# A macaron block on one core: waits between scattered stores, and the order of the router's steps around attention and the first shared products

## The reference, cut to what matters

```python
x = x + 0.5 * ffn(layernorm(x))
x = x + attention(layernorm(x))          # chunked gated linear attention, 2 heads of 128
x = x + 0.5 * ffn(layernorm(x))

def ffn(x):                              # 1024 tokens of 256 values
    shared = (silu(x @ g.T) * (x @ u.T)) @ down.T * sigmoid(x @ sgate.T)   # 704 hidden
    p = softmax(x @ gate.T)              # 16 experts
    w, ids = top_k(p, 4)
    return shared + sum over the 4 chosen experts e of  w_e * expert_e(x)  # 176 hidden
```

## Time and profile before

| | us |
|---|---|
| median of 3 runs | 455.74 (454.93 to 457.75) |
| the profiled execution's own time | 455.48 |
| its span, from first to last instruction | 453.7 |

### The profile page before, as it was taken

One profiled execution on the slowest core, in us unless ns is written; L12 is line 12 of the kernel. 1 busy time (PEld: TensorE's weight loads), 2 busy tenths in 40 slices (PEclk: granted clock), 3 DMA queues, 4 the chain that ended last, 5 costly groups with the idle time before them and its releaser, 6 DMA issues.

```text
span 453.7 us, 8744 instructions
## 1 busy us (share of the span) xinstructions
PE 410.8 (91%) x2236; PEld 330.4 (73%) x2239; DVE 300.4 (66%) x943; ACT 202.1 (45%) x564; POOL 188.9 (42%) x199
## 2 busy tenths in 40 slices
PE   5998993699999999978969989689989999999995
PEld 3555552599999999553649975355569999999954
DVE  5666986377777776367596545645767777777637
ACT  2224562266666666124755632001126666666610
POOL 0174846044445445330055300767514544544542
PEclk9988997699999999989998976989999999999999
DMA  7999941344444441660000029422244444444167
GB/s 248 332 281 386 344 136 66 105 136 139 136 148 137 138 144 66 245 252 2 0 0 1 1 73 372 170 104 103 79 119 137 136 138 148 132 145 141 68 242 258
DMA packets 41023, 68.17 MB, mean 150 GB/s; under 512 B 5072, under 2 KB 32208, under 8 KB 40976
## 3 DMA queue, kind: packets, MB, share of 16 engines
q1 hardware_dynamic: 33392, 45.84, 32.4%
q0 software_dynamic: 7584, 21.77, 13.6%
HBM read 42.42 MB, written 25.17 MB: 149 GB/s over the span
## 4 chain that ended last, share of the span: by engine, by line
PE 70%; issue 7%; POOL 6%; DVE 6%; DMA 6%; ACT 3%; SPq 1%; DVEq 0%; POOLq 0%
PE ps L486 7%; PE ps L487 7%; PE ps L490 7%; POOL slots L907 6%; PE ps L426 6%; PE ps L449 5%; PE ps L471 5%; PE ps L431 4%; PE ps L519 3%; PE ps L514 2%; PE ps L518 2%; PE ps L516 2%; PE ps L515 2%; PE ps L497 2%; PE ps L498 2%
## 5 line engine op out<-in xcount | busy, mean ns | idle before, releaser
L914 POOL DMA_INDIRECT rows<-ar,idx x94 | 89.8, 955 | 118.0 <-ACT ar L762 117.4
L907 POOL DMA_INDIRECT slots<-XR,pos x64 | 70.1, 1096 | 76.5 <-DVE pos L1084 41.6
L486 PE MATMUL ps<-WH,xt 128*128 x188 | 69.2, 369 | 0.0
L487 PE MATMUL ps<-WL,xt 128*128 x188 | 61.1, 327 | 0.0
L1127 DVE SCALAR_TENSOR_TENSOR ar<-ps,XR,ar 128x112 f32<-128x112 f32 x94 | 31.4, 334 | 37.9 <-ACT ar L756 37.7
L1143 DVE TENSOR_TENSOR xl<-ps,xt 128x256 fp32r<-128x256 f32 x94 | 39.9, 424 | 24.2 <-ACT xt L751 10.6
L449 PE MATMUL ps<-WS,ar 128*128 128x256 f32 (+1 forms) x192 | 48.4, 399 | 8.1 <-DVE ar L996 7.4
L449 PEld LDWEIGHTS ps<-WS,ar 128*128 128x128 f32 (+1 forms) x192 | 37.3, 197 | 24.7 <-issue 12.9
L756 ACT ACTIVATE ar<-ps 128x176 f32<-128x176 f32 x94 | 29.9, 318 | 51.5 <-PE ps L490 51.5
L426 PE MATMUL ps<-XT,WS 128*128 128x512 f32 x96 | 50.8, 656 | 1.0 <-ACT sgt L739 1.0
L745 ACT ACTIVATE ar<-ps 128x512 f32<-128x512 f32 (+1 forms) x24 | 14.3, 596 | 80.3 <-PE ps L426 80.3
(11 more groups left out here) (171 smaller groups left out, 855.3 us busy)
## 6 DMA issues: line engine op xcount, KB each, us to landing
XR<-slots SPq DMA_DIRECT2D x94, 144.0 KB, 2.1
WR<-w SPq DMA_DIRECT2D x8, 1408.0 KB, 17.1
WR<-rows SPq DMA_DIRECT2D x16, 512.0 KB, 7.3
slots<-zeros SPq DMA_DIRECT2D x1, 2304.0 KB, 12.6
MR<-w2r SPq DMA_DIRECT2D x2, 1024.0 KB, 19.3
MR<-w2m SPq DMA_DIRECT2D x1, 1792.0 KB, 14.3
rows<-ar,idx POOLq DMA_INDIRECT x94, 2.4
X<-x SPq DMA_DIRECT2D x4, 256.0 KB, 4.6
```

The lines of the kernel that those rows point to most:

```text
L486: pe.matmul(to, token, WH[:, bass.ds(e, 1), k, :].rearrange("p a n -> p (a n)"), start=k == 0, stop=False)
L487: pe.matmul(to, token, WL[:, bass.ds(e, 1), k, :].rearrange("p a n -> p (a n)"), start=False, stop=False)
L907: pool.indirect_dma_start(out=slots_dram[:, :], out_offset=bass.IndirectOffsetOnAxis(ap=pos[:, t, r:r + 1], axis=0), in_=XR[:, t, :], in_o ...
L914: pool.indirect_dma_start(out=rows_dram[:, :], out_offset=bass.IndirectOffsetOnAxis(ap=idx[:, i:i + 1], axis=0), in_=ys[i % NY], in_offset ...
```

## The change

Dispatch waits before each tile for the stores of the tile two before it, on one of two semaphores by the tile's parity; `BREAKS` is gone. `judge(1, 0)` and `router(1, 0)` move into attention's last loop. In the front, `ranks(f, 0)` goes between the two products of unit 0, PE does unit 2's input before `ranks(f, 1)` and unit 3's before `over_partitions`; DVE does unit 0 before `choose(f, 1)`, unit 1 before `places(f, 1)`, units 2 and 3 before `tables`; `places(0, 0)` goes ahead of the four scalings.

```diff
-BREAKS = (3, 6)
+        s_disp = [sem(f"s_disp{b}") for b in range(2)]
@@ SP, ahead of the slots' loads
-                sp.wait_ge(s_disp, 16 * NT * TOPK * (f + 1))
+                for b in range(2):
+                    sp.wait_ge(s_disp[b], 16 * TOPK * HT * (f + 1))
@@ PE
-            def unit_in(f, u):
+            def unit_in(f, u, between=None):
...
                 mm.then_inc(s_ug, 1)
+                if between:
+                    between()
@@ PE, ffn
-                unit_in(f, 0)
-                ranks(f, 0)
+                unit_in(f, 0, lambda: ranks(f, 0))
...
                 unit_in(f, 1)
                 unit_out(f, 0)
+                unit_in(f, 2)
                 ranks(f, 1)
-                unit_in(f, 2)
                 unit_out(f, 1)
+                unit_in(f, 3)
+                unit_out(f, 2)
                 over_partitions(f)
-                for u in range(3, FRONT):
+                for u in range(4, FRONT):
@@ ACT, attention
                 for i in range(3, NT + 5):
                     step(i)
-                router(1, 0)
+                    if i == NT + 2:
+                        router(1, 0)
@@ POOL, dispatch
-                        if t in BREAKS:
-
-                            pool.wait_ge(s_disp, 16 * TOPK * (NT * f + t))
+                        wait(pool, s_disp[t % 2], 16 * TOPK * (HT * f + t // 2))
                         for r in range(TOPK):
                             pool.indirect_dma_start(
                                 out=slots_dram[:, :], out_offset=bass.IndirectOffsetOnAxis(ap=pos[:, t, r:r + 1], axis=0),
-                                in_=XR[:, t, :], in_offset=None).then_inc(s_disp, 16)
+                                in_=XR[:, t, :], in_offset=None).then_inc(s_disp[t % 2], 16)
@@ DVE, ffn
+                unit(f, 0)
                 choose(f, 1)
-                unit(f, 0)
+                unit(f, 1)
                 places(f, 1)
                 tiles_of(f)
-                unit(f, 1)
-                tables(f)
-                for u in range(2, NJ + 1):
+                unit(f, 2)
+                part(f, 2)
+                for u in range(3, NJ + 1):
                     unit(f, u)
+                    if u == 3:
+                        tables(f)
                     part(f, u)
@@ DVE, attention's last loop
                         scale(2, i - 4)
-                judge(1, 0)
+                    if i == NT + 1:
+                        judge(1, 0)
                 choose(1, 0)
@@ DVE, ahead of ffn(0)
             choose(0, 0)
+            places(0, 0)
             for t in range(HT, NT):
                 scale(0, t)
-            places(0, 0)
```

More of the change, by code:

```diff
@@ L239, in macaron @@
         s_mv, s_ln, s_rs, s_xn, s_tp, s_xc = (sem(n) for n in "s_mv s_ln s_rs s_xn s_tp s_xc".split())
-        s_lg, s_lgc, s_ex, s_sgx, s_sel, s_rank, s_pos, s_disp, s_dg, s_tp4, s_tab, s_chain = (
-            sem(n) for n in "s_lg s_lgc s_ex s_sgx s_sel s_rank s_pos s_disp s_dg s_tp4 s_tab s_chain".split())
+        s_lg, s_lgc, s_ex, s_sgx, s_sel, s_rank, s_pos, s_dg, s_tp4, s_tab, s_chain = (
+            sem(n) for n in "s_lg s_lgc s_ex s_sgx s_sel s_rank s_pos s_dg s_tp4 s_tab s_chain".split())
         s_ug, s_uu, s_usi, s_uh, s_u2, s_xsh = (sem(n) for n in "s_ug s_uu s_usi s_uh s_u2 s_xsh".split())
+        s_disp = [sem(f"s_disp{b}") for b in range(2)]
         s_xs = [sem(f"s_xs{i}") for i in range(NX)]
```

## The result

The changed kernel took 478.71 us (median of 4 runs, 474.96 to 484.48), the kernel before 455.34 us beside it (4 runs, 454.60 to 457.75): a ratio of 1.048, 95% interval 1.038 to 1.057. The forecast was 443.4. The time is outside the range and on the wrong side of no change.

What follows compares the result with a forecast made beforehand. Dispatch was taken to bound both fronts: 32 spaced store issues and two full drains each. 455.48 - 7.5 (first front) - 4.8 (second) = 443.2 us profiled, given as 443.4 median; range 439.5 to 448.5.

Steps and rivals of the forecast that it cites:

- The waits: POOL's dispatches: dropping drains removes 9.0 and 2.9 us idle; new waits add 1 us in the first, nothing in the second.
- forecast's own signs of being wrong: Gap over 2 us at tile 4 or later, first-front DVE sums ending after 79, or attention's last tile turned later.
- D: Rival: in the first dispatch six waits cost 4.3 us each, POOL loses 26 us, time 467; chance 0.04.
- E: Rival: PE still stands for DVE in second front, first hidden behind DVE's weights; gain 3 + 1, 451.7; chance 0.06.
- First dispatch, start: Start of first dispatch: `places(0, 0)` passes four scalings, so it begins 1.25 us earlier.
- First dispatch, end: Last issue at 68.7; DVE is late next, its front ends at 77.1; first slot gains 7.5 us, bounds 5.5 and 9.
- Judging inside attention: Attention's last loop: `judge(1, 0)` adds tile 7 some 0.5 us later, covered by 2.8 us of slack; cost nothing.
- Second dispatch: Second front: starts 1.9 us earlier, drains give 2.9, still last; gain 4.8 us, bounds 3.0 and 7.1.
- rival C: Idle 2.34 us ahead of tile 7 goes, DVE's front is quicker: 9 + 7.1 gained, 439.6; chance 0.1.
- PE in the second front: Stands of 3.10 and 2.13 us go, one of about 0.5 stays; PE's front ends 6.2 us earlier, near 325.4.
- Sum: Whole kernel: 455.48 - 7.5 - 4.8 = 443.2 us for the profiled execution, 443.4 for the median.
- The clock: Second slots: PE would stand about 3 us after its warm-up products; a single stand of 3.1 us costs nothing.

Runs made afterwards that it cites:

- e17: The changed kernel itself, unaltered, on chip 9: 436.76 us beside 449.25 for the kernel before, ratio 0.978.
- e1: The kernel before with only the new waits on two semaphores, old order of work, chip 6: 476.56 us beside 456.95, ratio 1.047.
- e2: The changed kernel with the old two drains and one semaphore, new order kept, chip 6: 451.75 us beside 456.95, ratio 0.988.
- e15: The same kernel as e2, run again on chip 6: 452.96 us beside 455.37 for the kernel before, ratio 0.992.
- e7: The changed kernel with drains before tiles 3 and 6 in the second dispatch only, chip 3: 443.36 us beside 449.62, ratio 0.981.
- e8: The changed kernel with one drain per dispatch, before tile 4, chip 3: 440.57 us beside 449.62, ratio 0.984.
- e9: The changed kernel itself, unaltered, on chip 13: 479.87 us beside 450.54 for the kernel before, ratio 1.062.
- e4: The changed kernel with a full drain before every tile, chip 6: 470.79 us beside 456.95 for the kernel before, ratio 1.034.
- e14: The changed kernel plus 2 us of scratch fills before each tile but the first, chip 6: 455.77 us beside 455.37, ratio 1.001.
- e13: The changed kernel itself, unaltered, on chip 6: 483.53 us beside 455.37 for the kernel before, ratio 1.061.
- e3: The changed kernel with its two semaphores but full drains only, before tiles 3 and 6, chip 6: 452.43 us beside 456.95, ratio 0.988.

## Why the prediction was wrong

**The step that failed** is in *The waits*: the two drains go as "removed idle" of 9.0 and 2.9 us, and "Queued behind a waiting store on POOL are only later stores". Both look at what a pause costs POOL and those who wait for it. No step asked what an engine that never pauses does to engines that wait for none of its stores. The term was put at nothing without a reason. In the first result POOL's gain came, and the late waits cost 12.7 + 13.2 us plus the gains of 7.5 and 4.8: about 38 us. The same kernel's two profiled executions give this directly: first slot 97.32 against 76.12 in e17, and from attention's last tile to the second first slot 81.36 against 58.66, in sum 43.9 for the 43.3 us between their spans. Of the forecast's own signs of being wrong one came: DVE's sums of the first front end at 95.75 + 1.66 = 97.4, not before 79.

**The rivals didn't hold it either.** D, the slower one, had POOL's waits as its mechanism, 4.3 us at each of six; the longest in the first dispatch was 0.94. It had the sign and the wrong cause. E's "PE still stands for DVE" is nearer, but it left a gain of 4 us, not a loss of 23. The trace of the kernel before holds no late wait, so no row named this; but it also had no more than 12 stores in a row, and the forecast took all its prices from there to 32.

**Where no wait is late, the total came out, in part by luck.** e17 against the earlier trace rows, term by term:

```profile
30.77 0.96 POOL L908 DMA_INDIRECT slots<-XR,pos  x1 [0.87 <-DMA slots<-XR,pos]
...
61.77 0.97 POOL L908 DMA_INDIRECT slots<-XR,pos  x1 [1.78 <-DMA slots<-XR,pos]
...
311.60 1.02 POOL L908 DMA_INDIRECT slots<-XR,pos  x1 [0.30 <-issue]
```
```profile
74.55 1.65 DVE L1025 SCALAR_TENSOR_TENSOR X<-ps,gate,X 128x256 f32<-128x256 f32 x4
76.12 0.74 DVE L1144 TENSOR_TENSOR xl<-ps,xt 128x256 fp32r<-128x256 f32 x2
```

- *First dispatch, start*: 19.91 for 21.14, 1.23 earlier (forecast 1.25).
- *The waits*, added: 0.57 at tile 2 and 1.48 at tile 7 above the usual 0.30, in sum 2.05 us (forecast 1, bounds 0 to 2.7 each at tiles 2 and 3). The second one was not at a tile I had named. The last store ends at 68.75, where 68.7 + 0.96 was forecast: another idle piece of 2.34 us, in the kernel before's first dispatch too (72.39, tile 7), went and made up for it.
- *First dispatch, end*: the first slot is at 76.12, right behind DVE's sums, as forecast for 77.1: gain 8.5 for 7.5. ("Only half of what POOL wins" in the forecast is a slip: by its own numbers it was 7.5 of 9.25.) ACT did wait for its last weights, 4.75 us, but nothing behind it was late for that.
- *Judging inside attention*: attention's last tile is added 183.03 us after the first slot in both kernels, so it costs nothing, as forecast.
- *Second dispatch*: it begins 11.0 us after that tile in place of 15.79: 4.8 gained, not 1.9. Part of this is the clock of PE in these two executions: unit 0's gate product took 1.96 us in e17 and 3.76 before. In e1 and e2 the old and the new order stand 1.7 apart (10.34 and 8.64), near the 1.9 forecast. It takes 42.47 us for 47.22, 4.75 less: the drains' 2.9 and, of the 2.34 us ahead of tile 7, the 2.04 above the usual gap, which is rival C's term. That idle piece goes with the old dispatch: e2 and e15 have it too at tile 7 of both dispatches (2.33 to 2.35), no run with two semaphores has. From the last tile to the second first slot the gain is 9.5 us, forecast 4.8.
- *PE in the second front*: no stand of over 1 us up to the one before the slots (forecast one of 0.5, for 3.10 and 2.13 before).
- *Sum*: 12.5 us between the medians on chip 9, forecast 12.3; between the spans 18.0 (453.7 and 435.7), but these two need not be of one chip, and the terms above compare them too. So the terms add up to 18.0 us and not to 12.3, the second one at twice its forecast; that the medians differ by 12.5 doesn't confirm each of them. No trace of the kernel before on chip 9 exists to tell which of them shrinks there.

**The clock.** PE stood before the second slots in e17 as expected, 2.02 us for 3:

```profile
316.90 0.41 PE L472 MATMUL ps<-cst,XR 128*128 128x128 f32 x2 [2.02 <-issue]
...
318.00 0.42 PE L487 MATMUL ps<-WH,xt 128*128 x1
```

The product behind the stand takes 0.42 us, that of the kernel before's slots too, and the granted clock is 1.00 from 317 to the end in e17, and from 335 before. So this single stand cost no clock, as the forecast read from its row (3.10 us, then products at full speed).

**The better version.** None of those tried is best on all chips. The changed kernel gains most where no wait is late (0.978 on chip 9), though e7 and e8 on chip 3 (0.981 and 0.984) can't be told from it. Where they are, the new order with the old drains is the best seen (0.988 and 0.992 on chip 6, with two semaphores 0.988), and no other form was faster than before there; it wasn't run on the other chips. One drain at tile 4 gains 1.6% on chip 3 and nothing on chip 13.

## What to carry to other kernels

Before a pause is taken out of an engine that issues its stores by hand, ask what the other engines do in it, also those that wait for nothing of that engine; on some chips a stream of issues without a gap holds up the others, which no row of the old profile prices. Read a wait by its producer's end, its semaphore's update and its own start, not by the releaser's name: "remote" in a program of one core, and a fall in the number of semaphore records, are the marks. And time a change of this kind on more than one chip: here the same kernel was 2.2% faster on one and 6% slower on two.

## What the runs showed of the hardware

- While POOL issues one indirect store per 1.26 us, the update of a semaphore by PE can be recorded, and the Silu that waits for it begin, up to 26.7 us after PE's product is over (e9: 304.58 and 331.26, the update at 331.24). DVE's updates come late too (1.29 us, L1102 to L1103). Seen in 9 of the 11 runs on chips 6 and 13 (the other two, e4 and e14, pause before every tile) and in the first result, in none of the 7 on chips 3, 9 and 15, of which e17 issues as densely. Every trace with late waits also lacks about 2,000 of 6,870 records of semaphore updates; e4's and e14's lack 1,400 and 1,600.
- A pause of 2.0 us before every four stores removed all late waits behind gate products on chip 6 (28 us between e13 and e14), without a wait for the stores just issued. Drains did the same when there was one per tile (e4), and most of it at two per dispatch (e2, e3, e15: up to 10.1 us left).
- The late updates don't need stores in flight: in the first result's second dispatch the stores' queue is empty for 0.67 to 0.75 us between every two stores from 302 us on, and waits of 19.9 and 27 us pass through that stretch.
- An idle piece of 2.34 us ahead of a store of tile 7, with no reason in the profile, stands in both dispatches of the kernel before, e2 and e15, which have the old dispatch, and in none of the runs with two semaphores.
- A few stores took 2.4 to 2.9 us to issue in place of 0.96 (five over 1.2 us of 32 in the first dispatch before, seven in e17; the longest of all runs is 5.64, in e15). In the changed kernel's first trace, where DVE mostly stood, the longest of all 64 was 1.15.
